# A two-layer attention and feed-forward kernel: the tail of its last batch split by halves of 128 rows

## What is computed

```
x = x + attn0(gate(x, side))      # normalised attention, both softmaxes
x = x + ffn0(gate(x, side))       # one fp8 product with bias
x = x + attn1(gate(x, side))      # causal attention with rotary positions
x = x + ffn1(gate(x, side))       # the stage of this case

def ffn1(x):                      # w1: 1024 x 256, w2: 256 x 1024, both ternary
    h = bitlinear(x, w1)          # every row of x scaled by 127 / max|row|, rounded, clipped
    return bitlinear(square(relu(h)), w2)
```

## Time and profile before

| | us |
|---|---|
| median of 3 executions | 330.92 |
| lowest, highest | 330.6, 331.57 |
| the profiled execution, its own time | 331.89 |
| its span, first to last instruction | 330.1 |
| TensorE, VectorE, ScalarE busy in the span | 274.2, 253.9, 204.9 |

### The profile page before, as it was taken

How to read it: one execution, slowest core, us unless ns; L and a number is a source line. 1 busy time by engine, 2 the same in 40 slices (tenths; PEclk the granted TensorE clock), 3 DMA queues, 4 the chain that set the end, 5 groups by cost and what they waited for, 6 DMA issues and landing times.

```text
span 330.1 us, 6222 instructions
## 1 busy us (share of the span) xinstructions
PE 274.2 (83%) x2400; PEld 165.3 (50%) x2400; DVE 253.9 (77%) x492; ACT 204.9 (62%) x348; POOL 38.7 (12%) x63
## 2 busy tenths in 40 slices
PE   7789697697999979676689799879788987988755
PEld 2244353464665636343436556556445754565423
DVE  1869939557999989869959998995886577755771
ACT  3756829548999798835533954776307684574531
POOL 1200111111112212030100114410040000000000
PEclk9699758769999999999969859998959999999998
DMA  5930141533377565021030363363051000000010
GB/s 128 390 134 2 38 90 20 110 66 66 66 133 218 98 130 113 18 41 23 6 61 0 65 128 65 67 127 66 0 103 27 0 18 16 3 2 23 10 34 32
DMA packets 8237, 22.55 MB, mean 68 GB/s; under 512 B 1552, under 2 KB 2960, under 8 KB 7824
## 3 DMA queue, kind: packets, MB, share of 16 engines
q0 software_dynamic: 4032, 14.68, 23.8%
q1 hardware_dynamic: 4176, 7.48, 6.5%
HBM read 6.43 MB, written 1.05 MB: 23 GB/s over the span
## 4 chain that ended last, share of the span: by engine, by line
PE 51%; DVE 24%; issue 10%; ACT 9%; DMA 3%; POOL 1%; DVEq 0%; ACTq 0%; POOLq 0%
PE PS L1421 6%; PE PM L1229 4%; PE PO L1174 4%; PE PO L1189 3%; PE PS L1159 3%; PE PM L1338 3%; PE PO L1436 3%; PE PM L1132 3%; DVE kp L976 3%; DVE fwd L735 2%; PE PO L1198 2%; PE PM L1119 2%; PE PS L1514 2%; PE PO L1537 2%; PE PM L1489 2%
## 5 line engine op out<-in xcount | busy, mean ns | idle before, releaser
L533 ACT ACTIVATE E<-PS,negc,escale 128x1024 f32<-128x1024 f32 x32 | 38.3, 1199 | 10.5 <-PE PS L1159 10.5
L976 DVE TENSOR_REDUCE kp<-PS 128x2 f32<-128x256 f32 x64 | 32.3, 549 | 13.7 <-PE PS L1400 13.5
L657 ACT ACTIVATE E<-PS 128x384 f32<-128x384 f32 x64 | 27.8, 488 | 23.2 <-PE PS L1421 23.2
L332 POOL DMA_DIRECT2D fwd<-mid x14 | 12.2, 872 | 108.7 <-DVE fwd L735 108.7
L1159 PE MATMUL PS<-TP 32*128 32x256 f16 x256 | 20.6, 286 | 2.8 <-DVE TP L780 2.8
L1174 PE MATMUL PO<-E,kp 128*32 128x256 f32 x256 | 18.9, 416 | 3.9 <-ACT E L533 2.1
L338 POOL DMA_DIRECT2D fwd<-bwd x14 | 12.4, 884 | 73.4 <-DMA fwd<-mid 42.5
L1338 PE MATMUL PM<-G,sg 128*128 128x512 f32 x32 | 18.3, 705 | 2.0 <-DVE sg L753 2.0
L745 DVE TENSOR_TENSOR_SCAN bwd<-ek,DT 128x511 f32<-128x511 f32 x16 | 19.8, 1236 | 0.0
L735 DVE TENSOR_TENSOR_SCAN fwd<-DT,ek 128x512 f32<-128x512 f32 x16 | 19.5, 1217 | 0.0
L735 DVE TENSOR_TENSOR_SCAN fwd<-DT,ekv 128x512 f32<-128x512 f32 x16 | 19.4, 1211 | 0.0
(11 more groups left out here) (216 smaller groups left out, 610.9 us busy)
## 6 DMA issues: line engine op xcount, KB each, us to landing
fwd<-mid POOLq DMA_DIRECT2D x14, 512.0 KB, 4.6
fwd<-bwd POOLq DMA_DIRECT2D x14, 512.0 KB, 4.5
kT<-in_kT SPq DMA_DIRECT2D x4, 256.0 KB, 6.8
xT<-in_xT SPq DMA_DIRECT2D x4, 256.0 KB, 5.4
G<-in_w SPq DMA_DIRECT2D x1, 1024.0 KB, 9.8
vt<-in_w SPq DMA_DIRECT2D x1, 1024.0 KB, 11.6
G<-in_attn SPq DMA_DIRECT2D x1, 1024.0 KB, 6.8
out<-ek SPq DMA_DIRECT2D x8, 128.0 KB, 1.7
```

Source lines behind the costliest of these rows:

```text
L533: nc.scalar.activation(E[:, p % 6], PS[:, 2 * (p % 2):2 * (p % 2) + 2, :], ACT.Exp, bias=negc[:], scale=escale[:]).then_inc(S["e0_done"], 1)
L657: nc.scalar.activation(E[:, p % 4, i, 0:384], PS[:, i, 0:384], ACT.Exp, scale=QSCALE).then_inc(S["e1_done"], 1)
L976: nc.vector.tensor_reduce(kp[:, b % 2, u * H + 2 * j:u * H + 2 * j + 2, D], PS[:, at0:at0 + 2, lo:hi], AX, ALU.max, negate=True).then_inc( ...
```

## The change

Up to slot 31 both programs are the same. From slot 32 on they differ:

- **Batch 3 by halves.** State, projection, tanh, gating, largest value, scales, rounding, turning and copy are done for tile 6 and then for tile 7, 256 columns at a time. The halves' projections go to PM bank 1 and PM bank 0.
- **Tiles 6 and 7 by halves of their 1024 columns.** `relu` and `square` are split in two of 512 columns; `last_factor` makes the scale from both largest values.
- **Who does what.** Rounding by scale (`last_round`, `last_hidden_q`) is done by ScalarE for batch 3 and tiles 6 and 7, in place of VectorE. The copies of the turned hidden rows of tiles 6 and 7 (`last_turned_copy`) are done by VectorE in place of ScalarE.
- **More banks.** Turns of tiles 4 to 7 go to PS 0, PM 0, PO 1, and PS 0 with PS 1; products of tiles 3 to 7 go to PO 0, PM 1, PS 2, PS 3 and PO 1, so `down` no longer waits for the `final` before it.
- **Order.** `down` and `final` of tile 3 move from slot 33 to behind the projection, and the `final`s of tiles 3 to 7 all stand at the end of VectorE's list. `whole` is issued 12 times in the tail as before, at other places. The two slots of `otile` and the stores are as before.

TensorE at the start of the tail, before: from the last turn of the attention's rows to the projection.

The diff, without the tables and without functions that are only cut in half:

```diff
...
+        HID_AT = (17, 19, 25, 27, 31, 33)
+        SQUARE_AT = (17, 19, 25, 27, 33)
...
+            def last_round(u):
+                act.wait_ge(S["tail_scaled"], u + 1)
+                nc.scalar.activation(xrnd[1][:, u], sg[:, seg(LAST, u * C, C)], ACT.Copy, scale=fs[:, LAST, 3, u:u + 1],
+                                     bias=ROUND).then_inc(S["tail_round"], 1)
+
+            def turned_rows_copy(t, src):
+                act.wait_ge(S["hqtr_done"], t + 1)
+                act.wait_ge(S["ffn1_done"], t - 1)
+                nc.scalar.activation(hqT[t % 2], src.bitcast(BF16), ACT.Copy, bias=-128.0).then_inc(S["hqT_done"], 1)
...
+            def last_hidden_q(u, n):
+                act.wait_ge(S["tail_factor"], u + 1)
+                act.wait_ge(S["tail_square"], 2 * u + n + 1)
+                if n == 0:
+                    act.wait_ge(S["hqtr_done"], 2 * LAST + u - 1)
+                nc.scalar.activation(hqb[u][:, HALVES[n]], hsq[u][:, HALVES[n]], ACT.Copy,
+                                     scale=fs[:, LAST, 10, u:u + 1], bias=128.0).then_inc(S["tail_hq"], 1)
+
+            turned_rows_copy(4, PS[:, 0, :])
+            last_tanh(0)
+            square(5)
+            last_tanh(1)
+            last_round(0)
+            last_state(0)
+            last_state(1)
+            last_round(1)
+            for n in range(2):
+                last_square(0, n)
+            turned_rows_copy(5, PM[:, 0, :])
+            for n in range(2):
+                last_hidden_q(0, n)
+            for n in range(2):
+                last_square(1, n)
+            for n in range(2):
+                last_hidden_q(1, n)
...
-                dve.wait_ge(S["x3_done"], b + 1)
+                dve.wait_ge(S["x3_done"], b + 1 + (t == TILES - 1))
                 if t >= 2:
                     dve.wait_ge(S[f"stored{t % 2}"], 16 * (t // 2))
-                nc.vector.scalar_tensor_tensor(otile[:, t % 2], PO[:, 1 if t < 4 else 0, 0:C], fs[:, b, 11, u:u + 1], x3tok[b][:, u],
+                src = (PO[:, 1], PO[:, 1], PO[:, 1], PO[:, 0], PM[:, 1], PS[:, 2], PS[:, 3], PO[:, 1])[t]
+                nc.vector.scalar_tensor_tensor(otile[:, t % 2], src[:, 0:C], fs[:, b, 11, u:u + 1], x3tok[b][:, u],
...
+            def last_turned_copy(i, src, at):
+                dve.wait_ge(S["tail_hturn"], i + 1)
+                dve.wait_ge(S["ffn1_done"], 2 * LAST - 1 + (i > 0))
+                nc.vector.tensor_scalar(hqT[i > 0][:, at], src, -128.0, None, ALU.add).then_inc(S["tail_hcopied"], 1)
+
+            last_gated(0)
+            last_largest(0)
+            last_scale(0)
+            last_gated(1)
+            last_rows(0)
+            last_largest(1)
+            last_rows_copy(0)
+            last_scale(1)
+            hidden_q(5)
+            last_relu(0, 0)
+            last_rows(1)
+            last_relu(0, 1)
+            last_rows_copy(1)
+            last_scales()
+            last_factor(0)
+            last_relu(1, 0)
+            last_relu(1, 1)
+            last_factor(1)
+            final(3)
+            last_turned_copy(0, PO[:, 1, :].bitcast(BF16), slice(0, HID))
+            final(4)
+            for n in range(2):
+                last_turned_copy(1 + n, PS[:, n, 0:T].bitcast(BF16), HALVES[n])
+            for t in range(5, TILES):
+                final(t)
 
 
...
+            def turn_late(t, bank):
+                pe.wait_ge(S["hq_done"], t + 1)
+                for k in range(HID // P):
+                    ins = nc.tensor.transpose(bank.bitcast(BF16)[:, k * P:(k + 1) * P], hqb[t % 2][:, k * P:(k + 1) * P],
+                                              identb[:])
+                ins.then_inc(S["hqtr_done"], 1)
+
+            def down_late(t, bank):
+                for k in range(HID // P):
+                    if t == TILES - 1 and k % 4 == 0:
+                        pe.wait_ge(S["tail_hcopied"], 2 + k // 4)
+                    ins = nc.tensor.matmul(bank[:, 0:C], hqT[t % 2][:, k * P:(k + 1) * P], w2q[:, k * C:(k + 1) * C],
+                                           start=(k == 0), stop=(k == HID // P - 1))
+                ins.then_inc(S["ffn1_done"], 1)
...
+                if p in (32, 33):
+                    last_state(p - 32)
                 if p in (23, 24, 25, 26, 27):
                     pe.wait_ge(S["g3_done"], 2)
                     whole(PM[:, 0], 2)
-                if p in (36, 38, 40, 41):
-                    pe.wait_ge(S["g3_done"], B)
-                    whole(PM[:, 0], 3)
...
+
+            pe.wait_ge(S["e1_done"], 2 * B * PAIRS)
+            turn_late(4, PS[:, 0, :])
+            whole(PS[:, 1, :], 1)
+            for u in range(TT):
+                last_project(u)
+            pe.wait_ge(S["po1_free"], PO1["hidden", 3] + 1)
+            pe.wait_ge(S["y1_done"], B * CH)
+            down_late(3, PO[:, 0, :])
+            whole(PS[:, 1, :], 2)
+            last_turn_x(0)
+            last_hidden(0)
+            pe.wait_ge(S["hqT_done"], 1)
+            pe.wait_ge(S["x3_done"], LAST + 1)
+            down_late(4, PM[:, 1, :])
+            pe.wait_ge(S["x3_done"], LAST + 2)
+            turn_late(5, PM[:, 0, :])
+            whole(PS[:, 1, :], 2)
+            last_turn_x(1)
+            last_hidden(1)
+            pe.wait_ge(S["tail_relu"], 2)
+            whole(PS[:, 3, :], 2)
+            pe.wait_ge(S["hqT_done"], 2)
+            down_late(5, PS[:, 2, :])
+            whole(PS[:, 3, :], 2)
+            pe.wait_ge(S["tail_xcopied"], 2)
+            last_turn(0, 1, PO[:, 1, :], 0, 8)
+            whole(PS[:, 3, :], 2)
+            pe.wait_ge(S["tail_relu"], 4)
+            for n in range(2):
+                last_turn(1, n, PS[:, n, :], n * 512, 4)
+            whole(PS[:, 3, :], 1)
+            pe.wait_ge(S["tail_hcopied"], 1)
+            down_late(6, PS[:, 3, :])
+            down_late(7, PO[:, 1, :])
```

More of the change, by code:

```diff
@@ L245, in build @@
         ROT_AT = (-PAIRS, -PAIRS, 0, 1, 7, 8, 15, 16)
-        SLOTS1 = range(-PAIRS, DOWN_AT[-1] + 1)
+        SLOTS1 = range(-PAIRS, TURNY_AT[-1] + 1)
+        LAST = B - 1
+        HALVES = [slice(n * 512, (n + 1) * 512) for n in range(2)]
         def max_bank(n):
@@ L266, in downs @@
         def downs(p):
-            return len([t for t in range(4) if DOWN_AT[t] < p])
+            return len([t for t, at in enumerate(DOWN_AT) if at < p])
         PO1, DOWN_USES = {}, {}
@@ L1105, in _, with last_gated, last_largest @@
                     behind(n, 0)
+            def last_gated(u):
+                rows = sg[:, seg(LAST, u * C, C)]
+                dve.wait_ge(S["tail_tanh"], u + 1)
+                dve.wait_ge(S["g3_done"], B)
+                link(nc.vector.scalar_tensor_tensor(rows, rows, 1.0, G[3][:, seg(LAST, u * C, C)], ALU.add, ALU.mult))
+            def last_largest(u):
+                f = fs[:, LAST, :, u:u + 1]
+                link(nc.vector.tensor_reduce(f[:, 0], sg[:, seg(LAST, u * C, C)], AX, ALU.max, apply_absolute_value=True))
@@ new lines, in last_hidden @@
+            def last_hidden(u):
+                pe.wait_ge(S["tail_xcopied"], u + 1)
+                if u == 0:
+                    pe.wait_ge(S["relu_done"], 2 * LAST)
+                else:
+                    pe.wait_ge(S["hqT_done"], 1)
+                for n in range(2):
+                    for k in range(HALF):
+                        ins = nc.tensor.matmul(PS[:, (2, 0)[u] + n, :], xqT[LAST][:, u, k, :],
+                                               w1q[:, k * HID + n * 512:k * HID + (n + 1) * 512],
+                                               start=(k == 0), stop=(k == HALF - 1))
+                    ins.then_inc(S["tail_hid"], 1)
@@ L1541, in _, with last_turn @@
+            def last_turn(u, n, bank, at, count):
+                pe.wait_ge(S["tail_hq"], 2 * u + n + 1)
+                for k in range(count):
+                    ins = nc.tensor.transpose(bank.bitcast(BF16)[:, k * P:(k + 1) * P],
+                                              hqb[u][:, at + k * P:at + (k + 1) * P], identb[:])
+                ins.then_inc(S["tail_hturn"], 1)
             for p in SLOTS1:
```

97 lines of the change are left out of this document (81 added, 16 removed).

## The result

| | before | after |
|---|---|---|
| median of 4 executions each | 330.76 us | 319.51 us |
| lowest, highest | 329.37, 331.57 | 317.26, 322.04 |
| the profiled execution: span, own time | 330.1, 331.89 | 317.5, 319.28 |

What follows compares the result with a forecast made beforehand. The tail was taken as a chain of latencies on three engines: 3.0 us gained by first gating, 1.6 in the middle, and after the end's store wait 6.2 in all, from median 330.92 to 324.7; range 323.8 to 327.5.

Steps and rivals of the forecast that it cites:

- 6.2 us off the median of 330.92: Whole kernel: the profiled span's forecast gain, 330.1 to 323.9, taken off the base median to give 324.7.
- both programs are one up to slot 31: Everything ahead of the tail: the programs are the same there, so the forecast counts no gain.
- Start of the tail: From heads_out of the last four heads to first gating: gating starts at 306.0 instead of 309.02, 3.0 us gained.
- Middle: First gating to last last_factor: VectorE's list is the bound, 9.9 us instead of 11.5, 1.6 us more gained.
- End: Last roundings to last final: tile 7's final waits for tile 5's store, ends at 321.7; span 323.9.
- The copy at double rate: VectorE's copy of tile 6's 1024 bf16 columns from PSUM: 0.69; at single rate 0.5 longer, span 324.3.
- The stores: Rival at the end: bunched stores land after 3.1 us, holding the finals; gain 2.6, median 328.3; chance 12%.
- The clock in the tail: Rival: TensorE at half clock from 313 gives gain 4.2; plain runs before lacking the low stretch, 4.8; chance 15%.
- the 1.4 us that hung on it: End of the old tail: the part of the 6.2 us gain that depends on TensorE's lower clock there.
- Slower: Rival: TensorE at half clock through the whole tail from 304; span 334.8, 4.7 more, median 335.6; chance 4%.
- table loads: Rival: ScalarE table load (1.28) between tanh and squares or rounding, two places; gain 3.6, median 327.3; chance 3%.
- level: Rival: the chain ends within 0.3% of before, by waits not seen; chance 3%.

Runs made afterwards that it cites:

- e12: Kernel after with four result slots, no tail constants, tile 7's second rounding half on VectorE, 15 constant products added in the first part: median 315.81 us, ratio 0.9723.
- e9: Kernel before with product and final of tile 3 moved behind the projection (slot 33 to 35): 330.40 us in one execution, tail 36.08.
- e6: Kernel after with the rounding (last_hidden_q) of tiles 6 and 7 back on VectorE: 325.09 us in one execution, tail 29.28.
- e8: Kernel after without its 12 constant products (whole) in the tail: 318.85 us in one execution, tail 26.99.
- e4: Kernel after with four slots for the results in place of two: median 317.65 us, ratio 0.9702, tail 26.40.
- e7: Kernel after with the three turned copies of tiles 6 and 7 back on ScalarE: 316.22 us in one execution, tail 27.29.
- e5: Kernel before with tile 7's turn and three constants ahead of tile 6's product, in banks of their own: 319.18 us in one execution, tail 31.99.
- e1: Kernel before run again with no edit: median 325.91 us, ratio 1.0022, tail 35.36.
- e3: Kernel before with 13 unused semaphores and ten constant products at the end of TensorE's list: median 327.80 us, ratio 1.0137, tail 33.92.

## Why the prediction was wrong in its number and right in its steps

Forecast were 324.7 (range 323.8 to 327.5), measured 319.51. **The step that failed** is "6.2 us off the median of 330.92", and with it "both programs are one up to slot 31", read as: both take the same time up to there. Over the 14 profiles, 13 of them with the same code up to there, the start of the shared copy goes from 285.4 to 296.1 and follows the lower clock ahead of it: the line through them rises 0.39 us for each us of lower clock and leaves 1.1 us of scatter (correlation 0.93). The profile of before had the most of all, 58.0 us; that of after 41.0. The line gives 6.6 for these 17 us, and 6.05 were measured. That the clock is the cause, and not only a companion, is what e12 speaks for: it adds work to TensorE ahead of the copy and nothing else, and its executions are shorter. What decides the clock stays open.

The three executions of before lay within 1 us of each other and made this look like a firm number. Over 42 of the 44 executions of the unedited kernel before (without 417.15 and 597.8) the mean is 326.8 (320.8 to 331.7), over the 14 of the kernel after 319.7 (316.0 to 323.4). The difference is 7.2 +- 1.5 us, which agrees with the forecast of 6.2 and with the 6.54 of the profiles' tails. The first four executions of before lie at 329.37 or above, of the 38 later ones only seven do, so that occasion was slow for this kernel by more than such scatter; why is open. Set against 326.8, the forecast would have read 320.6, and the kernel after measured 319.51. Not the size of the gain was wrong but the base from which it was counted, and the range, which had no term for it.

**Start of the tail: right.** With the shared copy at 290.04 the forecast reads 297.05 for the turn and 299.95 for gating; measured were 297.01 and 299.94. e9 shows the first half of it alone: 1.44 at the turn. What splitting by halves gives at gating no run shows by itself.

**Middle: right.** The last `last_factor` was to end at 309.85 and ended at 309.79 (309.58 + 0.21). The halves of `relu` took 0.68 for 0.69, and gating 0.43 for 0.42. e6 shows what ScalarE's rounding of tiles 6 and 7 is worth, here and at the end together: 1.85.

**End: right, with errors that cancel.** `final` of tile 7 was forecast for 315.15 and came at 314.82, held by the store of tile 5 as written. A pair of ScalarE's roundings took 1.32 for 1.46, and the last ended 0.6 early; the constants, put at nothing because they lie in TensorE's free time, cost 0.45 (e8). The slots are worth 1.03 (e4), and the copies' move to VectorE -0.15 (e7), which the prediction's sum did not price as a step of its own. The order of turn 7 and product 6, with its banks, is worth 2.0 in the old tail (e5).

**The copy at double rate: right.** The subtraction over 1024 bf16 columns of PSUM took 0.68; the single rate would have been 1.2. The Trainium skill, VectorE: DVE Perf Modes, section The perf-mode tier table, allows PSUM sources double rate at most, and this row agrees. The Trainium skill, the same page, section The TRN2 errata, asks for tiles of at least 512 elements, because each instruction on SBUF pays a fixed part. This case's rows agree on the fixed part: two squares of 512 columns took 1.13 in a row, one of 1024 took 1.06. The whole tail still became shorter with halves of 512 and even of 256; how much of that the halves gave, and how much order and banks, no run separates.

**Rivals.** The stores: none landed after more than 1.7. The 3.1 of the earlier trace rows was tile 4's store, one with no other within 4.8 us of it, and the same store took 3.6 in e1 and 3.4 in e3 and in e5: it comes with the old order and not with bunched stores, and why is open. The clock in the tail: none lower in the three profiles of the kernel after. So the 1.4 us that hung on it should be in the gain; that size no run measures, and the rows show 0.84 of it (1.89 for the product of tile 6 against 1.05 for the next). Against e1, whose old tail had 10.6 us of lower clock, the gain would have been 7.9. Slower, table loads, level: did not come.

## What to carry to other kernels

Divide the span at the last instruction that both programs share, and compare behind it; the new tail agreed to 0.03 us in three executions (the old one to 1.4) while the identical part ahead of it moved by 10. A total says little below 2% until the clock in the unchanged part has been compared, and three executions that agree do not make a base. Where results leave through a few slots, count them before moving work between engines: here a copy cheaper by 0.9 us was worth nothing, because a store held the slot.

The kernel that the rows point to, four slots with the constants kept and the first part filled as in e12, was not run.
